# New engine orders for six attention layers and for a causal attention, and weights loaded one block earlier

## The reference

```python
# causal attention: q, k of 32 columns, v through a product of two small matrices,
# softmax over the earlier tokens, 4 batches of 512 tokens
x = x + ga * _L1_attn_ref(h, Wq, Wk, Wvdown, Wvup)
h = _layernorm(x, axis=-1) * (1 + cb) + sb
# six layers, 16 heads of 64, a window of 32 tokens behind each block
for i in range(6):
    x = attn_layer(shift_tokens(x), Wqkv[i], q_scale[i], k_scale[i], Wo[i]) + x
    x = ffn_layer(shift_tokens(x), ln_g[i], ln_b[i], W1[i], b1[i], W2[i], b2[i]) + x
```

## Time and profile before

| what | us |
|---|---|
| median of 3 runs | 2570.37 (2567.61 to 2574.81) |
| profiled execution, its own time | 2579.3 |
| its span | 2577.5 |
| causal attention, from the end of its layer norm to its last result | 711 to 768.7 |
| layer norm in front of the six layers | 769.0 to 782.5 |
| six layers | 782.6 to 2577.5 |

### The profile page before, as it was taken

One profiled execution on the slowest core, in us unless ns is written; L12 is line 12 of the kernel. 1 busy time (PEld: TensorE's weight loads), 2 busy tenths in 40 slices (PEclk: granted clock), 3 DMA queues, 4 the chain that ended last, 5 costly groups with the idle time before them and its releaser, 6 DMA issues.

```text
span 2577.5 us, 60504 instructions
## 1 busy us (share of the span) xinstructions
PE 2324.6 (90%) x22196; PEld 1667.1 (65%) x22196; DVE 1969.4 (76%) x4390; ACT 1848.1 (72%) x4176; POOL 1272.9 (49%) x1093
## 2 busy tenths in 40 slices
PE   6798699999864799999999999999999999999996
PEld 3476378888652566666666666666666666676663
DVE  2598477777765788888888888888888888887862
ACT  2255488888643688777788788888787788887872
POOL 0132000000003777776777777677777777776650
PEclk8899899999886899999999999999999999999997
DMA  2000111222002001112111211112111111111110
GB/s 84 9 2 1 44 69 73 74 74 74 18 1 90 24 22 39 40 39 55 30 33 38 55 32 25 41 38 55 38 41 38 41 37 38 33 38 52 28 28 21
DMA packets 37811, 103.90 MB, mean 40 GB/s; under 512 B 7952, under 2 KB 13392, under 8 KB 34704
## 3 DMA queue, kind: packets, MB, share of 16 engines
q1 hardware_dynamic: 37520, 100.04, 13.7%
...
## 4 chain that ended last, share of the span: by engine, by line
DVE 28%; PE 12%; POOL 8%; issue 8%; ACT 5%; DMA 5%; SPq 2%; POOLq 0%; ACTq 0%; DVEq 0%
DVE w_bb L1902 5%; DVE w_ab L1901 4%; DVE w_nrm L1908 4%; DVE w_sm L1924 4%; POOL w_ab L1993 4%; PE w_psP L1753 4%; DMA X<-tables_layer 3%; POOL w_ab L1998 3%; DVE w_mx L1918 3%; DVE w_nrm L67 2%; ACT w_pb L1853 2%; PE w_psF L1721 2%; POOL w_pb L2003 1%; PE w_psA L1786 1%; PE w_psF L1700 1%
## 5 line engine op out<-in xcount | busy, mean ns | idle before, releaser
L1993 POOL TENSOR_TENSOR w_ab<-w_ab,w_bb 128x512 f32<-128x512 f32 x384 | 490.3, 1284 | 175.9 <-DVE w_bb L1902 175.9
L1998 POOL TENSOR_TENSOR w_ab<-w_ab,w_nrm 128x512 f32<-128x512 f32 x384 | 395.6, 1044 | 105.7 <-DVE w_nrm L67 105.7
L1853 ACT ACTIVATE w_pb<-w_psS,w_mx 128x96 f32<-128x96 f32 x1536 | 392.2, 356 | 22.1 <-DVE w_mx L1918 21.1
L1901 DVE TENSOR_TENSOR w_ab<-w_psP,w_tabs 128x512 f32<-128x512 f32 x384 | 263.0, 685 | 165.3 <-ACT w_sq L1829 137.8
L1753 PE MATMUL w_psP<-w_hi,w_xh 128*128 128x512 f32 x576 | 297.1, 516 | 87.0 <-ACT w_v L1836 33.0
L2003 POOL TENSOR_TENSOR w_pb<-w_pb,w_sm 128x768 f32<-128x768 f32 x192 | 282.2, 1470 | 149.0 <-DVE w_sm L1925 149.0
L1829 ACT ACTIVATE w_sq<-w_psP 128x512 f32<-128x512 f32 x384 | 235.1, 613 | 79.9 <-PE w_psP L1753 72.4
L1860 ACT ACTIVATE w_pT<-w_psA 128x512 f32<-128x512 f32 (+1 forms) x384 | 231.6, 603 | 45.1 <-PE w_psA L1786 44.4
L1902 DVE TENSOR_TENSOR w_bb<-w_psP,w_tabs 128x512 f32<-128x512 f32 x384 | 261.5, 681 | 0.0
L1908 DVE TENSOR_REDUCE w_nrm<-w_sq 128x8 f32<-128x512 f32 x384 | 254.2, 672 | 1.6 <-ACT w_sq L1829 0.9
L1760 PE MATMUL w_psT<-tables_all,w_ab 128*128 128x128 f32 x1536 | 241.5, 281 | 6.0 <-ACT w_qT L1842 3.4
...
## 6 DMA issues: line engine op xcount, KB each, us to landing
...
```

Source lines behind the costliest of these rows:

```text
L1853: last = act.activation(pb[k % 2][:, 4 * j + q, WIN * (k % 2):], psS[j][:, q * KEYS:(q + 1) * KEYS], ACT.Exp, bias=mx[:, 4 * j + q:4 * j + ...
L1901: dve.tensor_tensor(ab[:, k % 2, j, :].rearrange("p (h x d) -> p h x d", x=2, d=32), src, tab[0], ALU.mult)
L1993: pool.tensor_tensor(a, a, bb[:, i % 2, :], ALU.add).then_inc(s["ad"], 1)
L1998: pool.tensor_tensor(a, a, nrm[k // 2][:, 1, 8 * (i % 8):8 * (i % 8) + 8].unsqueeze(2).to_broadcast([128, 8, DH]), ALU.mult).then_inc(s["n ...
```

## The change

Three parts. In the six layers all five tables are replaced, each with the same units. The layer norm before them becomes part of `windowed_layers`: SyncE's first loads become a function `loads`, passed to `adaln` and issued in its block, and `adaln` uses the memory of `w_ab` for its `yn`. In causal attention the order of the loops over u changes on TensorE, ScalarE and VectorE. The removed tables stand in the kernel above; here they are left out.

```diff
--- before.py
+++ after.py
@@ -267,12 +267,13 @@
             ch.link(dve.tensor_copy(c.band_bf[:, :, :], c.band[:, :, :]))
 
 
-def adaln(c, layer, part, loads=None):
+def adaln(c, layer, part, loads=None, yn=None):
 
 
     nc, n = c.nc, f"n{layer}{part}_"
     NT = NB * TILES
-    yn = c.sb(n + "yn", [128, NT, D])
+    if yn is None:
+        yn = c.sb(n + "yn", [128, NT, D])
     stats = c.sb(n + "stats", [128, NT, 6])
     mv = c.sb(n + "mv", [128, NT, 2])
     rs = c.sb(n + "rs", [128, 3, NT])
@@ -1379,10 +1380,12 @@
             scores(2)
             pe.wait_ge(s["ve"], 2)
             for u in range(8):
-                by_keys(u)
                 if u + 3 < 8:
                     scores(u + 3)
-                attend(u)
+                by_keys(u)
+                if u:
+                    attend(u - 1)
+            attend(7)
 
         @block.scalar
         def _(act):
@@ -1421,10 +1424,10 @@
                     left(1)
             for u in range(8):
                 exponentials(u)
+                if u:
+                    evacuate(u - 1)
                 if u + 2 < 8:
                     left(u + 2)
-                if u:
-                    evacuate(u - 1)
             evacuate(7)
 
         @block.vector
@@ -1480,8 +1483,9 @@
                     diagonal(u + 1)
                     maximum(u + 1)
                 normalise(u)
-                if u:
-                    result(u - 1)
+                if u >= 2:
+                    result(u - 2)
+            result(6)
             result(7)
 
 
@@ -1545,6 +1549,36 @@
     scl = c.sb("w_scl", [128, 2, 4, DH])
     first = oT[:, 0:6, :].rearrange("p a b -> p (a b)")
 
+    names = ("wa", "wf", "tab", "scl", "z", "xst", "wd", "wh", "wl", "xh", "xl", "y", "xs", "p", "sq", "ab", "rs", "ad", "nm", "t", "te", "vx", "s", "mx", "e", "r", "pn",
+             "pt", "pte", "av", "ot", "f", "xf", "xsf", "yn", "xn", "gg", "hh", "out")
+    s = {k: c.sem("w_s_" + k) for k in names}
+    s_ve = [c.sem(f"w_s_ve{j}") for j in range(2)]
+    s_norm, s_sum, s_f = (c.sem("w_s_chain_" + k) for k in ("norm", "sum", "tail"))
+
+    def load_scl(sp, layer):
+        sp.dma_start(scl[:, layer % 2, :, :].rearrange("p k d -> p (k d)"),
+                     c.ins["qk_scales"][:, 4 * DH * layer:4 * DH * (layer + 1)].to_broadcast([128, 4 * DH])
+                     ).then_inc(s["scl"], 16)
+
+    def load_tail(sp, layer):
+        wait(sp, s["out"], layer * NB)
+        sp.dma_start(w_o[:, :, :], c.ins["w_o1"][layer]).then_inc(s["wf"], 16)
+        sp.dma_start(w_1[:, :], c.ins["w_ff1"][layer]).then_inc(s["wf"], 16)
+        sp.dma_start(w_2[:, :, :], c.ins["w_ff2"][layer]).then_inc(s["wf"], 16)
+        sp.dma_start(cols[:, :], c.ins["cols_w"][layer]).then_inc(s["wf"], 16)
+
+    def loads(sp):
+        sp.dma_start(first, c.ins["w_qkv1"][0]).then_inc(s["wa"], 16)
+        load_scl(sp, 0)
+        load_scl(sp, 1)
+        sp.dma_start(x_dram, c.X[:, :]).then_inc(s["xst"], 16)
+        load_tail(sp, 0)
+
+    with ExitStack() as inner:
+        outer, c.stage = c.stage, inner
+        adaln(c, 1, 1, loads, ab[:, :, :, :].rearrange("p a b c -> p (a b c)")[:, 0:T].rearrange("p (k c) -> p k c", c=D))
+        c.stage = outer
+
     psP = [c.ps(f"w_psP{j}") for j in range(2)]
     psT = c.ps("w_psT")
     psA = c.ps("w_psA")
@@ -1552,11 +1586,6 @@
     psO = c.ps("w_psO")
     psF = c.ps("w_psF")
 
-    names = ("wa", "wf", "tab", "scl", "z", "xst", "wd", "wh", "wl", "xh", "xl", "y", "xs", "p", "sq", "ab", "rs", "ad", "nm", "t", "te", "vx", "s", "mx", "e", "r", "pn",
-             "pt", "pte", "av", "ot", "f", "xf", "xsf", "yn", "xn", "gg", "hh", "out")
-    s = {k: c.sem("w_s_" + k) for k in names}
-    s_ve = [c.sem(f"w_s_ve{j}") for j in range(2)]
-    s_norm, s_sum, s_f = (c.sem("w_s_chain_" + k) for k in ("norm", "sum", "tail"))
 
     def ve_done(t, r):
 
@@ -1572,34 +1601,35 @@
 
     ORDER = {
         "pe": """
...
+            T3.0-- At2.0-- Av1.0-- V0.0- Av1.1-- S4.0-- T3.1-- At2.1-- back--- Av2.0-- V0.1- Av2.1--
+            P1.0- g0--- At3.0-- T3.2-- P1.1- S5.0-- P1.2- a0--- At3.1-- P1.3- g1--- T3.3-- Av3.0-- V1.0-
+            a1--- At4.0-- Av3.1-- V1.1- g2--- At4.1-- P2.0- Av4.0-- S6.0-- P2.1- T0.0- a2--- Av4.1--
+            T0.1- w2--- T0.2- At5.0-- P2.2- S7.0-- P2.3- T0.3- At5.1-- Av5.0-- V2.0- Av5.1-- At6.0--
+            T1.0- V2.1- S0.0- P3.0- T1.1- At6.1-- Av6.0-- P3.1- Av6.1-- At7.0-- T1.2- P3.2- At7.1--
+            Av7.0-- P3.3- S1.0- Av7.1-- V3.0- T1.3- At0.0- wo0-- V3.1- S2.0- P0.0 At0.1- T2.0- wo1--
+            P0.1 T2.1- S3.0- Av0.0- P0.2 T2.2- At1.0- tr-- T2.3- At1.1- Av0.1- P0.3""",
         "act": """
...
+            Te1.3-- Sq0.0- Xe2.0-- Xe2.1-- Te2.0-- Ve3.1-- xh0.0 Pt0.1-- Sq0.1- Te2.1-- Sq0.2- Te2.2--
+            Pt1.0-- Te2.3-- Xe3.0-- Pt1.1-- Ot0.0-- wh0.0- Xe3.1-- Te3.0-- Sq0.3- Pt2.0-- Ve0.0- Ot1.0--
+            Pt2.1-- xn--- Te3.1-- Xe4.0-- Ve0.1- Sq1.0- Xe4.1-- gg0--- Sq1.1- Te3.2-- Pt3.0-- Ot2.0--
+            Pt3.1-- Sq1.2- gg1--- Sq1.3- Xe5.0-- Pt4.0-- Ve1.0- Ot3.0-- Ve1.1- Te3.3-- Xe5.1-- gg2---
+            Sq2.0- Pt4.1-- Te0.0- Sq2.1- Xe6.0-- Te0.1- Xe6.1-- Ot4.0-- Pt5.0-- Sq2.2- Te0.2- Te0.3-
+            Pt5.1-- Sq2.3- Xe7.0-- Xe7.1-- Ve2.0- Ot5.0-- Pt6.0-- Te1.0- Ve2.1- Sq3.0- Te1.1- Pt6.1--
+            Xe0.0- Sq3.1- Ot6.0-- Pt7.0-- Xe0.1- Sq3.2- Pt7.1-- Te1.2- Sq3.3- Ot7.0-- Pt0.0- Xe1.0-
+            Xe1.1- Ve3.0-""",
         "dve": """
...
+            R3.0- AB3.1- R3.1- Xd0.0- AB3.2- R3.2- Xm1.0- Xm1.1- R3.3- AB3.3- Ra1.0- Xm2.0- tb0.0-
+            Xm2.1- Xd1.0- AB0.0 R0.0 Xd2.0- xf-- AB0.1 Xm3.0- Xm3.1- R0.1 AB0.2 ln-- AB0.3 Xm4.0- Xd3.0-
+            R0.2 Xm4.1- R0.3 R1.0 AB1.0 Xd4.0- Xm5.0- AB1.1 h0-- R1.1 AB1.2 Xm5.1- R1.2 AB1.3 h1-- R1.3
+            Ra0.0 Xm6.0- Xm6.1- Xd5.0- h2-- AB2.0 AB2.1 R2.0 Xd6.0- out-- R2.1 Xm7.0- AB2.2 Xm7.1- AB2.3
+            R2.2 Xd7.0- Xm0.0 Xm0.1 R2.3 AB3.0""",
         "pool": """
...
+            ad3.3-- nm2.1-- nm2.2-- nm2.3-- xl0.0 Xn1.0-- ad0.0- nm3.0-- ad0.1- Xn2.0-- nm3.1-- nm3.2--
+            ad0.2- nm3.3-- ad0.3- Xn3.0-- ad1.0- ad1.1- Xn4.0-- ad1.2- ad1.3- nm0.0- nm0.1- nm0.2-
+            Xn5.0-- nm0.3- ad2.0- Xn6.0-- ad2.1- nm1.0- ad2.2- ad2.3- nm1.1- nm1.2- Xn7.0-- wl0.0-
+            nm1.3- ad3.0- Xn0.0- ad3.1- ad3.2- nm2.0-""",
         "sp": """
...
+            VE1.0--- xfd---- VE2.0--- xd0.0 VE3.0--- VE0.0-- wd0.0- tl---""",
     }
 
     def unit(word):
@@ -1632,18 +1662,6 @@
     with nc.Block() as block:
         @block.sync
         def _(sp):
-            def load_scl(layer):
-                sp.dma_start(scl[:, layer % 2, :, :].rearrange("p k d -> p (k d)"),
-                             c.ins["qk_scales"][:, 4 * DH * layer:4 * DH * (layer + 1)].to_broadcast([128, 4 * DH])
-                             ).then_inc(s["scl"], 16)
-
-            def load_tail(layer):
-                wait(sp, s["out"], layer * NB)
-                sp.dma_start(w_o[:, :, :], c.ins["w_o1"][layer]).then_inc(s["wf"], 16)
-                sp.dma_start(w_1[:, :], c.ins["w_ff1"][layer]).then_inc(s["wf"], 16)
-                sp.dma_start(w_2[:, :, :], c.ins["w_ff2"][layer]).then_inc(s["wf"], 16)
-                sp.dma_start(cols[:, :], c.ins["cols_w"][layer]).then_inc(s["wf"], 16)
-
             def step(kind, k, j, r, b, layer):
                 if kind == "xd":
                     wait(sp, s["out"], r - NB + 1)
@@ -1658,7 +1676,7 @@
                         sp.dma_start(w_raw[:, :], c.ins["w_qkv1"][layer + 1][:, QTR * b:QTR * (b + 1)]).then_inc(s["wd"], 16)
                     if b == NB - 1 and layer < DEPTH - 2:
                         wait(sp, s["tab"], 4 * (layer + 1))
-                        load_scl(layer + 2)
+                        load_scl(sp, layer + 2)
                     if r == (DEPTH - 1) * NB + 1:
                         sp.wait_ge(s["p"], r * UP)
                         sp.wait_ge(s["xst"], 16)
@@ -1676,12 +1694,7 @@
                     sp.dma_start(xsf[64:128, 1:N], c.H[64:128, b * N:b * N + N - 1]).then_inc(s["xsf"], 16)
                 elif k == "tl" and b == 0:
                     if not isinstance(layer, int) or layer > 0:
-                        load_tail(layer)
-            sp.dma_start(first, c.ins["w_qkv1"][0]).then_inc(s["wa"], 16)
-            load_scl(0)
-            load_scl(1)
-            sp.dma_start(x_dram, c.X[:, :]).then_inc(s["xst"], 16)
-            load_tail(0)
+                        load_tail(sp, layer)
             sp.wait_ge(s["z"], 2)
             turns(sp, "sp", step)
             for b in range(NB):
@@ -2012,7 +2025,7 @@
         first = lambda: linear_attention(c)
         stages = [lambda: setup(c), first,
                   lambda: experts(c), lambda: causal_attention(c),
-                  lambda: adaln(c, 1, 1), lambda: windowed_layers(c, out)]
+                  lambda: windowed_layers(c, out)]
         for stage in stages:
             with ExitStack() as c.stage:
                 c.clears = stage is first
```

(14 more changed lines are left out.)

17 lines of the change are left out of this document (removed).

## The result

The changed kernel takes 2540.23 us (median of 4 runs, 2533.74 to 2547.27) where the kernel before takes 2571.21: 0.988 of it, 95% interval 0.985 to 0.991. The forecast was 2492 with a range from 2468 to 2534. The direction was right, the size was not: 31 us instead of 78. The profiled execution took 2536.73 us, its span is 2535.0.

What follows compares the result with a forecast made beforehand. TensorE's own work, 66.4 to 67.3 us a round, was taken as the floor, with waits and clock falls above it. 2579.3 - 63.4 - 1.5 - 10.4 - 8.1 = 2495.9, less 4: 2492 us, range 2468 to 2534.

Steps and rivals of the forecast that it cites:

- Step (a): SyncE's order in the six layers: wd moves behind VE0.0; Ve2.0 free 1.2 to 2.1 us earlier, clock falls gone.
- Step (b): Feed-forward tail: V3.1, S2.0, P0.0, At0.1 and T2.0 go between TensorE's wo halves, their PSUM banks free in time.
- Step (c): One new-order round walked with old durations: waits 0.8 at tr, 0.2 at T1.1, hand-overs 0.3; 67.7 us, 3.0 less.
- The fill: Start of the six layers, before 863 us: same chains in both orders, nothing gained, 8 us either way.
- Parts 2 and 3: Loads issued in the preceding layer norm: 10.4 us less (9 to 11); causal attention reordered: 8.1 less (5 to 9.5).
- E: Rival: the orders in the six layers bring nothing, they only shift waits; 2552 us; chance 0.04.
- B: Rival: half of it, VectorE or ScalarE become the pace in the six layers; round 69.2, 2525 us; chance 0.18.
- C: Rival: TensorE at its floor in the six layers, 66.6 us a round, 2471 us; chance 0.15.

Runs made afterwards that it cites:

- the three faults mended: Changed kernel with the tail's weights first, GpSimd quiet until the norm's reciprocal square root, Av halves side by side: 2478.80 us, 0.964 of the kernel before.

## Why the prediction was wrong, point by point

**What bounds the kernel: right.** TensorE's share, 66.4 to 67.3 us, was the floor of the old order, and the wait for the value rows with its falls of the clock stood above it: taken away alone it gave rounds of 67.9 with 66.7 of TensorE.

**Step (a), SyncE: right in mechanism and, alone, in size.** 0.6 and 0.6 to 1.5 us earlier, and the falls gone, were to bring most of the 3.0 us; alone it brought 2.4 a round (20 rounds of 70.8 to 20 of 68.4) and 48 us in all. Its end is false: I named VE1 and xfd as queued behind the blocked wd, and said that this costs nothing. The tail's four loads are queued there too, and cost 11 us.

**The sentence "the work of a round is the same, instruction for instruction; only positions change": this is the step that failed.** In these runs an instruction's time depends on its neighbours, on its own engine and on another one. On TensorE the floor is 66.4 plus six trips at 0.30 to 0.36, 68.2 to 68.6; measured 68.1. My walk priced "two Av together" at 1.08 to 1.15 also where the new order has them apart. On VectorE, GpSimd stood idle during the norm in the trace before, where L67 took 0.16 us in the mean; the new orders put GpSimd's products beside it, and the norm takes 8.1 us in the mean, from its first step to the end of its last, where it took 4.5 before and takes 4.8 with GpSimd held. The walk had `back` without a wait.

The sign stood in the trace before, in another root: the one of the head norms (Ra), whose first two steps, from 932 to 2348 us, were

```profile
L62 DVE SCALAR_TENSOR_TENSOR w_nrm<-w_nrm,w_halves 128x64 f32<-128x64 f32 x40 | 27.4, 685 | 0.7
L63 DVE SCALAR_TENSOR_TENSOR w_nrm<-w_nrm,w_guesses 128x64 int32<-128x64 int32 x40 | 22.4, 559 | 1.4
```

The changed kernel needs 221 and 225 ns for the same two. In the trace before one of these steps ends at 1418.83 and one at 1419.84, GpSimd's products at about 1418.76 and 1419.75. So more than half of the standing was moved, not made, by the new orders: over 20 rounds the norm's steps cost 73 us more, these two and the tables' products 40 us less. But TensorE waits for the norm.

**Step (b), the interleaved wo:** no wait there except for the late weights.

**Step (c), the walk:** the wait for `tr`, which I put at 0.8, was 0.82 in the round shown, but only seven of 20 rounds have one (7.8 us in all); `back` (1.1 us a round, 22.3 by 20) was not on my list. The round shown adds up: 68.1 of work, 0.82 at `tr` and 0.67 at `back` are 69.6 of its 69.7, where the forecast had 66.4 and 1.3. With the three faults mended the round takes 67.2, in the mean 67.5, near my 67.7. That is in part luck: its waits are 0.80 us in nearly each round for VectorE to read a projection's bank, which the walk had at nothing, and `tr` in four rounds of 20, which the walk had in each.

**The fill: mis-sized.** Nothing forecast, 7.9 us gained up to round 2, and 5.9 of the 13.0 in the table lie in the round behind it (69.3 to 63.4); the 20 rounds that follow gained only 0.36 us each, where 3.0 were forecast. The old orders in the new kernel fill in 132.0 us (first copy of x to the fourth), the new ones in 120.4. The new orders are better in this, and worse by 4 to 6 us behind the last copy of x (231.7 and 234.0 us against 227.7), where I had said that both orders have the same chains; I have taken neither apart.

**Parts 2 and 3: right in mechanism.** Part 2 gave 10.4 us, as forecast. The attention gave 9.8 for 8.1, a little beyond my bound of 9.5: its results 1 to 7 lie 18.0 us apart for my 18.8, and result 1 came 2.3 us earlier for my 1.4.

**The sum.** 2495.9 forecast for the profiled execution, 2536.7 measured. Of the 41 us missing, 50.4 are in the 21 rounds and 4.3 in the rest of the layers; 7.9 of the fill, 4.2 of the work before the attention's scores and 1.7 of the attention go the other way. Of the rivals, E (the orders only shift waits, 2552) came nearest, 12 us away, and had a chance of 0.04; the run with the old orders bears it out in the main, since the new ones brought 6 us; B (half of it, 2525) is 15 us away, and its reason was half right: VectorE did not run out of time by its work, but by standing for GpSimd inside its instructions. Neither had TensorE's own work growing, and C took it at its floor. The range ended at 2534 because I gave the terms of the walk no bound for prices that differ with the neighbour. The 0.94 for "faster" is also short: the forecast, B and C alone are 0.93, which leaves 0.01 for E where I wrote most of its 0.04. My own test line was right: rounds over 69 us with the wait for the value rows gone meant a higher floor than TensorE's share.

**What stays open.** Which waits of TensorE bring the clock down, and what in the new orders shortens the fill and lengthens the end of the block. The rounds of the best kernel vary between 67.2 and 68.4 us; four of its six longest have a wait of 0.7 to 1.1 us for the copy at `tr`, and why only these have it was not looked into.
